# Three passes of a four-layer attention model as one pipeline of 96 elements, weights exchanged in place, the maxima transposed 96 columns wide

## The reference, cut to what matters

```python
def layer0(x, ctx):                       # pass "l0"
    h = ln(x); q, k, v = split(h @ W_attn + b_attn)
    x = x + merge(softmax(mask_causal(q k^T * s)) v) @ W_aproj + b_aproj     # "own"
    x = x + merge(softmax(q' k'^T * s) v') @ Wcproj + bcproj                # "other", q' of ln(x), k', v' of ctx
    return x + gelu(ln(x) @ W_fc + b_fc) @ W_mproj + b_mproj                # "ff"

def layer1(x, ctx, mask):                 # pass "l1"
    x = ln(x + attention(x, x, x, mask) @ o_w + o_b)                        # "own"
    x = ln(x + attention(x, ctx, ctx) @ co_w + co_b)                        # "other"
    return ln(x + relu(x @ lin1_w + lin1_b) @ lin2_w + lin2_b)              # "ff"

def layer2(x, ctx, mask2):                # pass "l2", first half
    return ln(x + attention(x, ctx, ctx, mask2) @ wo)                       # "two"

def layer3(x, ctx):                       # pass "l2", second half, heads of 64
    return ln(x + attention64(x, ctx, ctx) @ w_fc)                          # "three"
```

## Time and profile before

| | us |
|---|---|
| median of 3 runs | 5057.91 (5057.47 to 5058.31) |
| the profiled execution | 5057.67 |
| its span, first to last instruction | 5055.6 |
| PE busy | 4791.4 (95%) |
| DVE busy | 3309.7 (65%) |
| ACT busy | 2626.5 (52%) |
| POOL busy | 1389.7 (27%) |

### The profile page before, as it was taken

One profiled execution on the slowest core, in us unless ns is written; L12 is line 12 of the kernel. 1 busy time (PEld: TensorE's weight loads), 2 busy tenths in 40 slices (PEclk: granted clock), 3 DMA queues, 4 the chain that ended last, 5 costly groups with the idle time before them and its releaser, 6 DMA issues. The chain is left out here.

```text
span 5055.6 us, 101677 instructions
## 1 busy us (share of the span) xinstructions
PE 4791.4 (95%) x36736; PEld 3797.7 (75%) x36800; DVE 3309.7 (65%) x10563; ACT 2626.5 (52%) x6913; POOL 1389.7 (27%) x1824
## 2 busy tenths in 40 slices
PE   5999999999998599999999999986999999999998
PEld 3788888888876367777777777764878778787786
DVE  3777777777774367677777767643656666565664
ACT  2556565565564144544444454533556565665655
POOL 2333333333331122333322322321122121211212
PEclk8999999999999699999999999997999999999999
DMA  4444444544442444343434344413221212212121
GB/s 127 134 133 120 141 127 119 147 123 123 140 120 59 126 121 121 114 131 105 139 104 130 114 127 119 121 50 99 65 73 52 71 56 66 72 52 71 54 68 30
DMA packets 393287, 513.56 MB, mean 102 GB/s; under 512 B 109136, under 2 KB 360784, under 8 KB 371280
## 3 DMA queue, kind: packets, MB, share of 16 engines
q1 hardware_dynamic: 384912, 495.52, 33.8%
q10 hardware_dynamic: 7872, 11.54, 0.7%
HBM read 266.30 MB, written 236.72 MB: 99 GB/s over the span
## 5 line engine op out<-in xcount | busy, mean ns | idle before, releaser
L550 POOL TENSOR_SCALAR l_veps<-l_meanvar 128x2 f32<-128x2 f32 x256 | 82.2, 321 | 1892.7 <-DVE l_meanvar L836 1892.7
L695 ACT ACTIVATE l_probs_own<-l_bank 128x384 f32<-128x384 f32 (+1 forms) x1024 | 479.0, 553 | 143.4 <-PE l_bank L1067 102.9
L628 ACT ACTIVATE l_ht<-l_bank,l_columns 128x256 f32<-128x256 f32 x384 | 197.7, 573 | 452.9 <-PE l_bank L1127 452.9
L769 ACT ACTIVATE l_probs<-l_bank,l_negmax 128x120 f32<-128x120 f32 x1024 | 355.1, 387 | 97.8 <-DVE l_negmax L1037 97.3
L935 DVE CUSTOM_DVE_ANT_0 l_bank<-l_bank,l_mask_rows 128x256 f32<-128x256 f32 x1024 | 396.3, 461 | 13.5 <-PE l_bank L1067 13.5
L1067 PE MATMUL l_bank<-l_kstack_own,l_qstack_own 96*128 96x256 bf16 (+1 forms) x2048 | 297.5, 264 | 42.5 <-DMA l_qstack_own<-q_parts 30.5
L1067 PE MATMUL l_bank<-l_qstack_own,l_kstack_own 99*128 99x256 bf16 (+1 forms) x2048 | 321.3, 263 | 14.9 <-DMA l_qstack_own<-l_nm_t_own 9.2
L695 ACT ACTIVATE l_probs_other<-l_bank 120x512 f32<-120x512 f32 x512 | 284.7, 613 | 73.7 <-PE l_bank L1067 70.8
L939 DVE TENSOR_REDUCE l_nmf_other<-l_bank 128x4 f32<-128x480 f32 x512 | 304.9, 646 | 7.6 <-PE l_bank L1067 5.5
L625 ACT ACTIVATE l_ct<-l_bank 128x240 f32<-128x240 f32 x96 | 35.6, 371 | 470.6 <-PE l_bank L1108 425.3
L1067 PEld LDWEIGHTS l_bank<-l_kstack_own,l_qstack_own 96*128 96x128 bf16 x2048 | 188.0, 99 | 110.0 <-DMA l_qstack_own<-q_parts 32.5
(11 more groups left out here) (247 smaller groups left out, 12431.2 us busy)
## 6 DMA issues: line engine op xcount, KB each, us to landing
l_kstack_own<-k_parts SPq DMA_DIRECT2D x64, 768.0 KB, 5.3
l_qstack_own<-q_parts SPq DMA_DIRECT2D x64, 768.0 KB, 7.3
l_qstack_other<-q_parts SPq DMA_DIRECT2D x64, 768.0 KB, 6.1
k_parts<-l_k_parts_own SPq DMA_DIRECT2D x64, 384.0 KB, 2.6
q_parts<-l_q_parts_own SPq DMA_DIRECT2D x64, 384.0 KB, 2.6
q_parts<-l_q_parts_other SPq DMA_DIRECT2D x64, 384.0 KB, 2.6
l_qstack_two<-q_parts SPq DMA_DIRECT2D x32, 768.0 KB, 6.5
l_kstack_other<-k_parts SPq DMA_DIRECT2D x64, 360.0 KB, 5.1
```

The lines of the kernel that those rows point to most:

```text
L550: nc.gpsimd.tensor_scalar(veps[key][:, :], meanvar[key][:, :, 1], norms[key]["eps"], None, ALU.add).then_inc(veps_ready.sem, 1)
L628: return nc.scalar.activation(out, in_, ACT.Identity, scale=scale, bias=bias)
L695: nc.scalar.activation(probs[key][0:rows, j % a.slots, 0:n], banks[bank_of[u.tag]][0:rows, 0:n], ACT.Exp, scale=a.scale).then_inc(a_done.s ...
L769: ins = nc.scalar.activation(probs3[:, j % 4, n, :], bank[:, n * S2:(n + 1) * S2], ACT.Exp, scale=-1.0, bias=negmax3[:, j, n:n + 1], accum ...
```

## The change

The three passes become one program (`run`) with one set of semaphores and one `nc.Block`. The steps of all 96 elements stand in one order for each engine. A step no longer has a lag and a bank but a position, in turns from the element's start; `Step` adds the element's number and the start of its pass, and each engine's list is sorted by the sum:

```diff
+PASSES = ("l0", "l1", "l2")
+START = {"l0": 0.0, "l1": 31.9145, "l2": 64.1522}
...
-            heads_t.own.0/2/7 ff_in.ff.3/4/4 scores_exp.other.4/3/2 scores_exp.other.1/3/0 scores_exp.other.6/3/6
...
+            norm.0.0/0.3211 project_k.own.0/0.4053 project_q.own.0/0.4453 project_v.own.0/0.7406 scores_max.own.3/0.9480
...
 class Step:
...
+        self.tag, self.of, self.element = (kind, key, int(j)), of, of * NB + i
+        name = PASSES[of]
+        later, wider = SPREAD[name].get(i, SPREAD[name].get(i - NB, (0.0, 1.0))) if kind not in ONCE else (0.0, 1.0)
+        self.at = START[name] + i + later + wider * float(at)
...
+def run(nc, passes, sb, t, ctx, mask_loads, make_masks):
+    plan = {e: [] for e in LISTS["l0"]}
+    for e, steps in plan.items():
+        for of, name in enumerate(PASSES):
+            for text in LISTS[name][e].split():
+                steps += [Step(text, of, i) for i in range(1 if text.split(".")[0] in ONCE else NB)]
+        steps.sort(key=lambda u: u.at)
```

```diff
+    free, holder, holds, done_by = [(0.0, b) for b in range(8)], {}, {}, {}
+    for u in plan["PE"]:
...
+        _, b = min(free)
...
+        holds[u.tag, u.element] = b, holder.get(b)
...
+        free[b] = when[by][read, u.element] + 0.02, b
```

```diff
+            if kind == "weights":
+
+                last, loads = r["weights"][key]
+                for count, tags, e in last({"a_full": a_full, "d_full": d_full, "ff_ready": ff_ready}):
+                    age = u.element - e
+                    tag = w.latest_first(count, tags, age)[0]
+                    if w.new(count, tag, age):
+                        act_e.wait_ge(count.sem, w.value(count, tag, age))
+                        settle(act_e)
+                for dst, src in loads:
+                    act_e.dma_start(dst, src).then_inc(arrived[key], 16)
...
+            ff_in.ff.0/3.9464 weights.own_qkv.0/-0.1540 weights.own_o.0/0.7346 weights.other_qkv.0/1.3081
+            weights.other_o.0/1.9510 weights.ff1.0/2.6199 weights.ff2.0/3.1321
```

```diff
-        nm_parts = each(atts, "nm_parts", [P, QT, PARTS, H], BF16)
+    each(KEYS, "nm_parts", [P, QT + 1, PARTS, H], BF16)
...
-                            ins = nc.tensor.transpose(bank[0:PARTS * H, t * P // 2:(t + 1) * P // 2].bitcast(BF16),
-                                                      nm_parts[key][:, t, :, :].rearrange("p a h -> p (a h)"), identb[:, :])
+                parts = nm_parts[key][:, :, :, :].rearrange("p t a h -> p (t a h)")
...
+                    ins = nc.tensor.transpose(bank[0:2 * PARTS * H, t * P // 2:(t + 1) * P // 2].bitcast(BF16),
+                                              parts[:, t * PARTS * H:(t + 2) * PARTS * H], identb[:, :])
```

2676 lines of the change are left out of this document (1392 added, 1284 removed), and 3 rows, old and new, of the table SPREAD.

## The result

The changed kernel takes 4904.36 us (median of 4 runs, 4901.68 to 4911.26) against 5058.11 of before in the same session: ratio 0.9697, 95% interval 0.9681 to 0.9714. It is faster by 154 us. The forecast was 4832 us, from 4795 to 4895: the direction is right, the size is 72 us short, and the time lies 9 us above the range. The profiled execution took 4902.52 us, its span 4900.7.

A forecast was written before the change was run, and what follows sets the result against it. PE's own work was taken as the bound, with time lost at the seams between passes. 5055.6 − 216 (overlap) + 18 (seams) − 28 (transposes) + 0 gave 4829.6 us of span, with 2.07 around it 4832 us; range 4795 to 4895.

The forecast's parts named there:

- The bound: In the three long stretches PE is busy nearly throughout at full clock, so its own work sets the pace.
- rivals 2, 4 and 5: 2: wider pair brings nothing, 4860, 17%; 4: shared-buffer wait brings seams back, 4978, 3%; 5: new banks slow each element, 3%.
- The seams, +18: Where passes meet: of the 216 us to be won, 18 us stay, bounded from 0 to 50.
- The 30 us for ACT's exchange of weights: At the seams: 12 ACT steps waiting for PE's last use of a weight delay up to 2.5 us each.
- the uneven second seam: Second seam: half turns alternate 15 and 33 us of matmuls; late work delays at most about 10 us each time.
- Rival 3: Seams close only in part, as PE stands before late steps: 86 us stay in place of 18, 4900 us; chance 14%.
- The wider transposes, −28: PE's transposes of the maxima: 96-wide pairs instead of 48-wide save 28 us, two thirds of 41.
- the full price: Wider transposes: the whole excess given back, 0.30 us a pair between f32 blocks and 0.19 between bf16 matmuls, 41 us.
- The cut of a third: Wider transposes: only two thirds of 41 us taken, since some freed time turns into waits for other engines.
- The start, 0: Pipeline fill: ACT's first norm between 19 and 37 us, DVE's masks 2.2 us late; net 0, from −5 to +13.
- the order inside a pass is the same: Within each pass: step order unchanged, so banks and waits cost 0, at worst 10 us.
- The third sign: In "l0": 8.17 instead of 8.07 matmuls a us would show that the wider transposes pay.

The follow-up runs named there:

- e7: e5 plus 161 bf16 matmuls whose result nobody reads, put ahead of ten waits of PE at the two seams; 4884.66 us.
- e9: Changed kernel with the start's transfers issued in order of need, each group when the DMA engines are idle, and DVE's masks later; 4882.76 us.
- e11: e9 plus the 161 unread matmuls of e7 at the seams; 4874.67 us.
- e6: e5 with all but the first masked-maxima instruction for a stack left out in the first four elements of "l1" (21.5 us of DVE's busy time); 4881.45 us, one execution.
- e13: e11 with half of DVE's masked maxima left out in the first four elements of "l1" and of "l2"; 4863.55 us, one execution.
- e6m: e5 with the same masked maxima left out as in e6, but in elements 10 to 13 of "l1", mid-pass, as a control; 4894.45 us, one execution.
- e4: Changed kernel with "l1" starting 0.1 turn later and "l2" 0.1 more; 4927.77 us, median of three.
- e14: e9 with "l2" placed 0.05 turns earlier; 4888.7 us, one execution.
- e10: e9 with 129 small moves of steps around the seams and the end, picked to avoid waits for inputs; 4894.36 us.
- e12: e11 with POOL held from two sums of "l1"'s last elements until DVE has split the last element's maxima; 4876.15 us.
- e15: e11 with PE's transposes of the maxima of "other" moved 0.01 turns earlier in elements 2 and 3 of "l0"; 4871.61 us.
- e5: Changed kernel with the last 19 of ACT's 35 first transfers issued ahead of the first exponentials, and DVE's "l1" masks behind the first split; 4893.52 us.

## Why the prediction was right or wrong

**The bound, right.** PE's work sets the pace: cut at the same events, "l0", "l1" and "l2" are within 0.5% of before. The mechanism of the change is right too: the waits of 28.7, 25.5 and 14.5 us are gone, and none of the rivals 2, 4 and 5 came.

**The seams, +18: the step that failed.** It is the term of the sum that was mis-sized: 67 us stay (39 and 28), above even its upper bound of 50. Three parts of its working failed.
1. The clock had no term. I counted what a full seam would take at the neighbours' rate, and bounded the rest by late steps, each at its own length. But in the first seam idle time was paid again: matmuls ran at the lower clock. e7 shows 9 us of it (6 from e9 to e11), where the clock rises from 0.94 to 1.00 once the idle time is filled. In the second seam, at 0.98, filling gave nothing.
2. DVE was held to be no bound because its mean is 78% and 72%. In the first seam it holds PE up by 8 us: that is what e6 gives, and e13 over e11, for a quarter less of its instructions, while e6m gives nothing. Its busy share would not have told. From 1660 to 1680 us, with "l1"'s maxima beside "l0"'s feed-forward steps, it is 94%; from 3000 to 3020, where PE loses nothing, 96%. That it counts whether PE has other work ready at that moment is likely and not shown.
3. The 30 us for ACT's exchange of weights, the larger part of the bound, were for nothing. ACT in the changed kernel, in the first seam:

```profile
1605.85 0.47 ACT L796 ACTIVATE ff_xu<-bank,columns_l 128x256 f32<-128x256 f32 x1
1605.97 0.37 ACTq L697 DMA_DIRECT2D w_other<-in_L_xattn_ck_w  x1
1606.21 0.48 ACT L797 ACTIVATE ff_xu<-bank,b_root 128x256 f32<-128x256 f32 x1
```

The issue goes out before ACT's instruction ahead of it has ended, and ACT's work runs on. Of the 12 steps that first wait for PE's last use, 11 begin to issue within a microsecond of the end of the instruction ahead. The twelfth (1722.63 us) begins 6.4 after it, and still 6.7 before ACT's next instruction, which waits for PE.

What filling and less DVE work don't explain is open: e13 still takes 222.4 and 331.7 us over the seams, 23 and 21 above the 199 and 311 of their matmuls. That it is each element's own chain, with fewer elements beside it to fill the time, is argued and not shown. e4 and e14 speak against the place of "l2", e10 against one set of small moves, e12 against POOL's part in the longest wait; POOL's part in the first seam, some 2 us, was not tried. The prediction's one exact place, the uneven second seam, was seen rightly (a half turn with 15 us of matmuls) and priced at 10 us; the 8.04 us wait stands there. It is the sum of the many short ones that was missing. Rival 3, with 86 us left, named this case and was given 14%. That its 4900 us lie so near the measured 4904 is in part luck: its seams would lose 19 us more than they did, and the transposes and the start 25 less.

**The wider transposes, −28: right mechanism, wrong size.** PE's busy time fell by 21.7 us, the span by 18 (15 by the medians of the runs), where the full price was worked out at 41. The pair's own 0.22 to 0.12 us came as forecast, and in "l2" the 1.73 us of the block ahead. What failed is the price of the rest: the block behind keeps 0.05 us and more, the block ahead in "own" of "l0" takes 1.79, and in "l1" half of the 0.19 comes back. That makes 27 us of the 41. The cut of a third for new waits was right in size (18 of 27), though only 3.6 us are seen to turn from busy time into waits.

**The start, 0: wrong, +12**, just inside its bound of +13. The parts: ACT's norm 3 us late, as its bounds allowed; with DVE's masks in the way (2.1 us, forecast 2.2) the first pair is 6.5 us late; of the 5.6 that the six turns behind it cost, 4.4 are in two of them. These contradict "the order inside a pass is the same": it holds in the middle of a pass, not for the elements that `SPREAD` moves. I took a statement on the middle for one on all.

**What would show.** The clock over the seams (0.94 and 0.98 and not 1.00) and 6.80 and 6.90 matmuls a us pointed at once to rival 3. The third sign, 8.17 matmuls a us in "l0", was badly chosen: the fixed stretch of 150 to 1500 us, 10834/1350 = 8.03 after, starts with the late elements of the start. From the 7th to the 32nd pair it is 9652/1199.94 = 8.04 before and 9655/1195.41 = 8.08 after, a rise of 0.4% where 1.2% was forecast: it said that the transposes fell short.

**The best version** by its median is e15, which e11 (4874.67) can't be told from with certainty: the loads spread by need, the idle time at the seams filled, one pair moved. 4871.61 us, 0.9629 (0.9612 to 0.9645) of before and 33 us below the changed kernel.

## What to carry to other kernels

When a barrier between two full pipelines goes, don't book the whole of its loss: here the first seam kept 39 of 126 us and the second 28 of 90, nearly a third each. In the first, 14 to 17 of the 39 are explained: an engine that is hidden in the middle of a pass (DVE) holds PE up where two passes meet, and a PE that idles for 4 us in 20 also works slower. An engine's busy share doesn't tell the two cases apart; leaving a part of its work out, in both places, does. Cut two traces at the same events, not at the same times, and a forecast's terms can be read off one by one. Loads that aren't due cost twice at this start, in the issuing queue and in the bytes beside the first transfer on the path.

## What the runs showed of the hardware

- **Unread matmuls pay.** 78 bf16 matmuls in the idle time of a 239 us stretch brought the granted clock from 0.94 to 1.00 and the stretch to 229.8 us. In the second seam, at 0.98, they gave nothing.
- **POOL and DVE.** DVE's CAST and TENSOR_TENSOR on 128x32 that write bf16 take 0.18 and 0.19 us alone and 1.12 to 1.21 beside POOL's TENSOR_TENSOR on 128x512. Of the 320 such instructions of the changed kernel 57 are that slow, each of them overlaps one of POOL's, and they end 0.04 to 0.05 us after it. By the Trainium skill, "SBUF — State Buffer", section "SBUF: two separate sides", the port pair that DVE and GpSimd share is an exclusive lock and the loser fully blocks; e12, where both are short again once POOL is held, agrees.
- **A stack among loads.** With the DMA engines at 101% PE waited 22.2 us for the first stack of 768 KB (e5), which landed 10.7 us after its issue. With fewer loads beside it (e9) it landed after 7.0, and PE waited 11.6.
- **A 96-wide bf16 pair among f32 blocks** costs, in "l2", nothing ahead of it and 0.05 us behind it, against 0.09 and 0.10 for a 48-wide one, and loads in 123 ns against 101.
